# Bias of queries and keys copied into PSUM by ScalarE ahead of the projection, statistics taken for two tiles at once, output projection one round later

## The reference

```python
def attention(x, Wq, bq, Wk, bk, Wv, bv, Wg, bg, Wo, bo):      # x: rmsnorm of the block's input
    q = phi(apply_rope(heads(x @ Wq + bq)))                     # phi(y) = elu(y) + 1
    k = phi(apply_rope(heads(x @ Wk + bk)))
    v = heads(x @ Wv + bv)
    g = heads(sigmoid(x @ Wg + bg))
    # chunks of 64 tokens, in order
    S = S + einsum('bhtd,bhte->bhde', kc, vc)
    Z = Z + kc.sum(axis=2)
    out = gc * (einsum('bhtd,bhde->bhte', qc, S) / (einsum('bhtd,bhd->bht', qc, Z)[..., None] + 1e-06))
    return out @ Wo + bo
```

## Time and profile before

| | |
|---|---|
| median of 3 runs | 2349.87 us (2348.94 to 2350.94) |
| the profiled execution | 2348.44 us, its span 2346.6 us |
| granted TensorE clock, mean over the span | 0.965 of full speed |
| busy over the span | PE 94%, PEld 82%, DVE 71%, ACT 38%, POOL 38% |
| first product of the attention (L1665, tile 0) | 794.00 us from the span's start |
| product L1665 of tile 5 (round 8) | 824.32 us |
| product L1665 of tile 9 (round 12, the first with every step) | 849.95 us |
| product L1665 of tile 31 (round 34) | 997.77 us |
| last score of the router kept | 1035.6 us |

### The profile page before, as it was taken

The page is one execution under the profiler, slowest core; times in us unless marked ns, Lnnn a source line. Parts: engine busy times, 40 slices in busy tenths (PEclk is TensorE's granted clock), DMA queues, the critical chain, the costliest instruction groups (busy, mean ns, idle before and its releaser), DMA issues. The chain is left out here.

```text
span 2346.6 us, 38035 instructions
## 1 busy us (share of the span) xinstructions
PE 2201.3 (94%) x13660; PEld 1929.2 (82%) x13660; DVE 1677.0 (71%) x3543; ACT 901.1 (38%) x1673; POOL 893.6 (38%) x925
## 2 busy tenths in 40 slices
PE   7998999999999599957999999969998999999998
PEld 5887888888889477746899999957887888888887
DVE  6775777777777588855766666646766777777776
ACT  5222333333333477732333333335222333333333
POOL 4211233333332599923444444443202332332332
PEclk9997999999999799968999999989998999999999
DMA  5003354354443411122334444352013444444442
GB/s 183 28 28 123 111 133 131 112 141 129 112 143 78 127 55 42 42 56 83 72 81 84 84 84 85 62 125 90 28 55 120 124 114 140 127 125 123 129 134 46
DMA packets 154108, 228.06 MB, mean 97 GB/s; under 512 B 33344, under 2 KB 104512, under 8 KB 153920
## 3 DMA queue, kind: packets, MB, share of 16 engines
q1 hardware_dynamic: 103664, 158.42, 21.5%
q0 software_dynamic: 39936, 55.93, 13.8%
q10 hardware_dynamic: 10320, 11.27, 1.4%
HBM read 171.16 MB, written 54.39 MB: 96 GB/s over the span
## 5 line engine op out<-in xcount | busy, mean ns | idle before, releaser
L1223 ACT ACTIVATE me_act_f<-me_in,me_bias 128x512 f32<-128x512 f32 (+1 forms) x192 | 119.0, 620 | 291.7 <-PE me_in L148 290.0
L1223 ACT ACTIVATE f2e_silu<-f2e_in,f2e_bias 128x512 f32<-128x512 f32 (+1 forms) x136 | 90.1, 663 | 341.5 <-PE f2e_in L148 293.6
L1223 ACT ACTIVATE f1e_silu<-f1e_in,f1e_bias 128x512 f32<-128x512 f32 (+1 forms) x136 | 90.2, 663 | 341.1 <-PE f1e_in L148 293.3
L146 PE MATMUL f1e_in<-f1e_xt_hi,f1e_w_hi 128*128 128x512 f32 (+1 forms) x544 | 208.9, 384 | 3.6 <-DVE f1e_xt_lo L1283 2.0
L146 PE MATMUL f2e_in<-f2e_xt_hi,f2e_w_hi 128*128 128x512 f32 (+1 forms) x544 | 208.8, 384 | 3.6 <-DVE f2e_xt_lo L1283 2.0
L148 PE MATMUL f2e_in<-f2e_xt_hi,f2e_w_lo 128*128 128x512 f32 (+1 forms) x544 | 208.1, 383 | 0.0
L148 PE MATMUL f1e_in<-f1e_xt_hi,f1e_w_lo 128*128 128x512 f32 (+1 forms) x544 | 207.9, 382 | 0.0
L147 PE MATMUL f2e_in<-f2e_xt_lo,f2e_w_hi 128*128 128x512 f32 (+1 forms) x544 | 207.7, 382 | 0.0
L147 PE MATMUL f1e_in<-f1e_xt_lo,f1e_w_hi 128*128 128x512 f32 (+1 forms) x544 | 207.5, 381 | 0.0
L146 PE MATMUL me_down<-me_w_hi,me_act_hi 128*128 128x256 f32 x640 | 183.4, 287 | 0.0
L147 PE MATMUL me_down<-me_w_lo,me_act_hi 128*128 128x256 f32 x640 | 179.7, 281 | 0.0
(11 more groups left out here) (460 smaller groups left out, 6996.2 us busy)
## 6 DMA issues: line engine op xcount, KB each, us to landing
f_raw<-in_ffn_w SPq DMA_DIRECT2D x256, 384.0 KB, 3.2
m_raw<-in_moe_w SPq DMA_DIRECT2D x64, 256.0 KB, 2.8
f1s_x_all<-in_x SPq DMA_DIRECT2D x8, 512.0 KB, 7.0
after_ffn<-f1s_out SPq DMA_DIRECT2D x8, 512.0 KB, 2.9
after_moe<-ma_x_all SPq DMA_DIRECT2D x32, 128.0 KB, 1.7
m_h<-ma_h SPq DMA_DIRECT2D x32, 128.0 KB, 1.7
f2s_x_all<-after_moe SPq DMA_DIRECT2D x8, 512.0 KB, 9.7
out<-f2s_out SPq DMA_DIRECT2D x8, 512.0 KB, 2.9
```

The source lines that it names most:

```text
L146: pe.matmul(out, lh, rh, start=first, stop=False, skip_group_check=True)
L1223: act.activation(dst[:, st % 2, 0:n], ps_in[st % 2][0][:, 0:n], func, bias=bias[:, b, f:f + 1]).then_inc(silu_done, 1)
```

## The change

The bias of queries and keys no longer comes from a product. ACT copies the bias row (held on all partitions) into `ps_qk` by the new step `set_bias`, and the six matmuls add to it. `set_bias` of tile r stands in the round before its projection, right behind `copy_qk` of tile r - 1, and takes over the wait for DVE's `rotate` of tile r - 1. One matmul of zeros over the bank at the start replaces the setting up of `pick` and `bias_rows`. Mean and variance are taken for two tiles in every second round, and POOL makes scale and shift for both in four operations (before: three for each tile), one round earlier. On PE `project_o` goes from lag 7 at the end of a round to lag 8 behind `turn_q`. On DVE the statistics go to the front, and `feature` goes behind `state1` and `state0`.

```diff
-            def root(r):
...
-                pool.tensor_scalar(mv[:, u, 2:3], mv[:, u, 1:2], EPS, None, ALU.add).then_inc(own_var, 1)
-                pool.wait_ge(own_var, r + 1)
-                pool.tensor_tensor(rs[:, u], mv[:, u, 1:3], neg_half[:], ALU.pow).then_inc(own_pow, 1)
-                pool.wait_ge(own_pow, r + 2)
-                pool.tensor_scalar(shift[:, u], rs[:, u], mv[:, u, 0:1], -1.0, ALU.mult, ALU.mult).then_inc(rs_done, 1)
+            def roots(r):
+                if r % 2 == 0:
+                    pair = slice(r % 4, r % 4 + 2)
+                    pool.wait_ge(stat_done, r + 2)
...
+                    pool.tensor_scalar(neg_mean[:, pair], mv[:, pair, 0], -1.0, None, ALU.mult)
+                    pool.tensor_scalar(mv[:, pair, 2], mv[:, pair, 1], EPS, None, ALU.add).then_inc(own_var, 1)
+                    pool.wait_ge(own_var, r // 2 + 1)
+                    pool.tensor_tensor(rs[:, pair], mv[:, pair, 1:3], neg_half[:], ALU.pow).then_inc(own_pow, 1)
+                    pool.wait_ge(own_pow, r // 2 + 2)
+                    pool.tensor_tensor(shift[:, pair], rs[:, pair], neg_mean[:, pair].unsqueeze(2).to_broadcast([P, 2, 2]),
+                                       ALU.mult).then_inc(rs_done, 1)
...
-            rounds([(10, row_roots), (1, root), (8, residual), (2, add_bo), (3, rotate)])
+            rounds([(10, row_roots), (0, roots), (8, residual), (2, add_bo), (3, rotate)])
...
+            pe.matmul(ps_qk[:], zeros[:, 0:P], zeros[:], start=True, stop=True).then_inc(qk_cleared, 1)
...
                 pe.wait_ge(at_done, r + 1)
-                if r >= 1:
-                    pe.wait_ge(rot_a_done, r)
-                pe.matmul(ps_qk[:], pick[:], bias_rows[:], start=True, stop=False, skip_group_check=True)
+                pe.wait_ge(bias_set, r + 1)
                 project(r, ps_qk, QK, qk_done)
...
-            rounds([(12, score), (6, turn_q), (7, numerators), (5, chunks), (6, last_chunk), (3, project_qk), (7, turn_o),
-                    (11, turn_h), (2, turn_a), (3, project_vg), (7, project_o)])
+            rounds([(12, score), (6, turn_q), (8, project_o), (7, numerators), (5, chunks), (6, last_chunk), (3, project_qk),
+                    (7, turn_o), (11, turn_h), (2, turn_a), (3, project_vg)])
...
+            def set_bias(r):
...
+                if r >= 1:
+                    act.wait_ge(rot_a_done, r)
+                act.copy(ps_qk[:], bias[:, QK]).then_inc(bias_set, 1)
...
-            rounds([(12, keep_score), (6, copy_qt), (4, exp_rot), (3, copy_qk), (7, copy_ot), (11, copy_ht),
-                    (2, split_at), (1, norm), (8, sum_squares), (10, normalise_h), (3, values)], after=(2, round_bias))
+            rounds([(12, keep_score), (6, copy_qt), (4, exp_rot), (3, copy_qk), (2, set_bias), (7, copy_ot), (11, copy_ht),
+                    (2, split_at), (1, norm), (8, sum_squares), (10, normalise_h), (3, values)])
...
-            rounds([(8, add_out), (0, stat), (7, divide), (4, feature), (6, state1), (5, state0), (3, rotate), (7, split_o),
-                    (2, split_low), (3, add_vg_bias)], after=(1, weights_low))
+            rounds([(0, stats_of_pair), (8, add_out), (7, divide), (6, state1), (5, state0), (4, feature), (3, rotate),
+                    (7, split_o), (2, split_low), (3, add_vg_bias)], after=(1, weights_low))
```

More of the change, by code:

```diff
@@ L1455, in attention @@
         wo_hi, wo_lo = s.sb("wo_hi", [P, K, D], F32R), s.sb("wo_lo", [P, K, D], F32R)
-        bias, bias_rows = s.sb("bias", [P, 4 * D]), s.sb("bias_rows", [P, 2 * D], F32R)
-        pick_f, pick = s.sb("pick_f", [P, P]), s.sb("pick", [P, P], F32R)
+        bias = s.sb("bias", [P, 4 * D])
         bo, rope = s.sb("bo", [P, D]), s.sb("rope", [P, Q, 4, DK // 2])
-        zeros, square = s.sb("zeros", [P, K * HW]), s.sb("square", [P, D])
+        zeros, square = s.sb("zeros", [P, 2 * D]), s.sb("square", [P, D])
         x_all, x2_all = s.sb("x_all", [P, T, D]), s.sb("x2_all", [P, T, D])
@@ L1498, in attention @@
                 "o_turned", "ot_done", "wo_done", "x2_done", "sum_done", "total_done"))
-        own_den, own_div, own_var, own_pow, own_ones, own_mean = (
-            s.sem(n) for n in ("own_den", "own_div", "own_var", "own_pow", "own_ones", "own_mean"))
+        own_den, own_div, own_var, own_pow, own_mean = (
+            s.sem(n) for n in ("own_den", "own_div", "own_var", "own_pow", "own_mean"))
         root2_done, h_done, h_turned, ht_done, score_done, score_kept, router_done, spare_out = (
@@ L1619, in _ @@
             for u in range(2):
-                pe.matmul(ps_state[u][:].rearrange("p k c -> p (k c)"), zeros[:, 0:P], zeros[:], start=True, stop=False,
+                pe.matmul(ps_state[u][:].rearrange("p k c -> p (k c)"), zeros[:, 0:P], zeros[:, 0:K * HW], start=True, stop=False,
                           skip_group_check=True)
+            pe.matmul(ps_qk[:], zeros[:, 0:P], zeros[:], start=True, stop=True).then_inc(qk_cleared, 1)
             pe.wait_ge(const_in, 16 * N_CONST)
@@ L1753, in _ @@
                 act.activation(w_hi[:, k], w_raw[:, k], ACT.Copy, scale=scale[:, k:k + 1]).then_inc(w_hi_done, 1)
-            def round_bias():
-                act.wait_ge(bias_in, 16)
-                act.copy(bias_rows[:], bias[:, QK]).then_inc(rows_rounded, 1)
+            def set_bias(r):
+                if r == 0:
+                    act.wait_ge(bias_in, 16)
+                    act.wait_ge(qk_cleared, 1)
+                if r >= 1:
+                    act.wait_ge(rot_a_done, r)
+                act.copy(ps_qk[:], bias[:, QK]).then_inc(bias_set, 1)
             def norm(r):
-                u = r % 2
-                act.wait_ge(rs_done, r + 1)
+                u, q = r % 2, r % 4
+                act.wait_ge(rs_done, r // 2 + 1)
                 if r >= 2:
                     act.wait_ge(a_turned, r - 1)
-                act.activation(x2_all[:, tile(r)], x_all[:, tile(r)], ACT.Identity, bias=shift[:, u, 1:2], scale=rs[:, u, 1:2])
-                act.activation(a[:, u], x_all[:, tile(r)], ACT.Identity, bias=shift[:, u, 0:1], scale=rs[:, u, 0:1]
+                act.activation(x2_all[:, tile(r)], x_all[:, tile(r)], ACT.Identity, bias=shift[:, q, 1:2], scale=rs[:, q, 1:2])
+                act.activation(a[:, u], x_all[:, tile(r)], ACT.Identity, bias=shift[:, q, 0:1], scale=rs[:, q, 0:1]
                                ).then_inc(a_done, 1)
@@ L1848, in _, with stats_of_pair @@
             dve.memset(v1[:], 1.0).then_inc(set_up, 1)
[L1849 to L1865, removed]
+            def stats_of_pair(r):
+                if r % 2 == 0:
+                    if r >= 4:
+                        dve.wait_ge(stat_done, r - 2)
+                    for i in (r, r + 1):
+                        dve.wait_ge(loaded(i), 16)
+                        dve.bn_stats(stats[:, i % 4], x_all[:, tile(i)]).then_inc(stats_done, 1)
+                    wait_apart(dve, stats_done, r + 2)
+                    if r >= 4:
+                        wait_apart(dve, a_done, r - 2)
+                    for i in (r, r + 1):
+                        dve.bn_aggr(mv[:, i % 4, 0:2], stats[:, i % 4]).then_inc(stat_done, 1)
             def split_low(r):
@@ L1957, in scale_router @@
                                       ).then_inc(router_done, 1)
[L1959 to L1962, removed]
             def weights_low():
```

20 lines of the change are left out of this document (7 added, 13 removed).

## The result

The changed kernel takes **2362.6 us** (median of 5 runs, 2359.1 to 2365.1) against 2349.0 us for the kernel before (median of 5, 2345.9 to 2350.9): ratio 1.0058, 95% interval 1.0044 to 1.0073, slower by 13.7 us. The forecast was 2356.3 us, range 2343 to 2363, slower with a chance of 0.56. The direction and the mechanism of the steady rounds were right; the loss was twice the forecast, and the median lies 0.4 us inside the upper end of the range.

What follows compares the result with a forecast made beforehand. POOL's list was taken as the bound, 13.45 us a pair of rounds, PE close behind at 13.02. Terms 7.5 + 1.0 + 1.2 - 0.7 - 2.5 = +6.5 us on the profiled 2348.44 gave a forecast median of 2356.3, range 2343 to 2363.

Steps and rivals of the forecast that it cites:

- steady rounds: Rounds 12 to 34 of the attention: 14.1 us a pair against 13.45, +7.5 us in all, between +5 and +10.
- What bounds the kernel now: In the attention, POOL's own list sets 13.45 us a pair of rounds; PE is close behind at 13.02.
- VectorE's loop: From rotate to rotate through set_bias, ACT's copies, split_at and DVE's list: 7.21 us in the round with statistics.
- TensorE's loop: From rotate to rotate through set_bias, copy_ot, copy_ht and PE's list with the moved project_o: 6.89 us.
- The price of the bias copy: set_bias on ACT, writing 128x512 into PSUM: 0.48 us until the next copy, bounds 0.38 and 0.60.
- Round 7: copy_ot of tile 0 comes behind rotate and set_bias, ahead of all of project_o's start: +1.2 us, bounds 0 and 2.
- The clock: Rival: PE waits some 0.6 us a round and its clock falls, +3 us a round, +70 in all; chance 0.02.
- Rounds 8 to 11: Attention rounds without score and copy_ht: 13.3 us a pair against 12.8, +1.0 us.
- The start: PE's bias_rows wait and slow product go, but the first norm awaits a second tile's statistics: -0.7 us, bounds -1.3 and +0.6.
- The tail: Behind the last projection, score and turn_q stand in PE's wait for split_o; four rounds, -2.5 us.
- the rival of a slowed VectorE: A DVE pass beside a long POOL operation slows the statistics round, +5 us on top: +11 to +16; chance 0.10.
- The faster rival: PE becomes the bound at 12.54 us a pair in the steady rounds: about -13 us, 2337; chance 0.20.

Runs made afterwards that it cites:

- E7: Kernel before with only the statistics and roots of two tiles at once, at the old place in VectorE's order; 2351.5 us, ratio 1.0004.
- E4: Kernel before with only project_o moved one round later, behind turn_q; 2343.7 us, ratio 0.9979.
- R1: Changed kernel run once more, unchanged, for its trace; 2362.9 us.
- R2: Changed kernel run another time, unchanged, for its trace; 2363.4 us.
- E1: Changed kernel with only set_bias moved on ScalarE, from ahead of copy_ot to behind split_at; 2338.0 us, ratio 0.9952.
- E8: Changed kernel with set_bias behind split_at and project_o back at its old place, the round's end; 2341.7 us, ratio 0.9961.
- E3: Kernel before with set_bias alone, ahead of copy_ot, in place of the bias product; 2370.3 us, ratio 1.0095.
- E2: Changed kernel with the bias product back on TensorE and no set_bias, the rest of the change kept; 2343.2 us, ratio 0.9968.
- E5: Changed kernel with set_bias between copy_ht and split_at on ScalarE; 2342.4 us, ratio 0.9968.
- E6: Changed kernel with set_bias between copy_ot and copy_ht on ScalarE; 2353.6 us, ratio 1.0012.

## Why the prediction was right or wrong

- *What bounds the kernel now.* Right: with GpSimd relieved alone (E7) the rounds went from 6.72 to 6.50 us, TensorE's 6.51 of the earlier trace rows. GpSimd's list was taken as fixed at 13.45 us a pair, and in E4 a pair takes 13.13 (910.53 to 923.66, from one L1571 to the second next).
- *The loops.* Right in kind and in place: ACT waits for `ma_rot_a`, DVE for `ma_ot_hi`, PE for `ma_ht`, the rounds alternate. VectorE's loop was 7.21 forecast, 7.16 measured. TensorE's loop was **6.89 forecast, 7.06 measured**, and that is the mis-sized term of the steady rounds: `project_o` at its new place takes 915.88 - 914.99 = 0.89 us until the next matmul against 0.71 taken from the round's end before, the bias copy 0.53 until the next copy against 0.48, `score` and `turn_q` 0.64 against 0.71. (The 0.27 of `copy_ot` is the row of `copy_ht` in the earlier trace rows, 920.06 - 919.79; its own row has 0.51 there. It measured 0.26.) A pair takes 14.25 us on average against 14.1 forecast and 13.45 before, and the 11 pairs between tile 9 and 31 cost 8.9 us, where 11 times the forecast 0.65 is 7.2 (the prediction counted 11.5 pairs).
- *The price of the bias copy.* 0.59 us, by its row L1761; 0.52 to 0.53 until the next copy, inside the bounds of 0.38 and 0.60. The Trainium skill, "ScalarE: Activation LUTs", section "ACT is a hardware spline evaluator", says that ScalarE reaches PSUM with less delay than SBUF. For this shape no run shows it: 0.59 into PSUM, 0.60 into SBUF.
- *Rounds 4 to 7* had no term and cost about 2 us. The loop over `split_at` was priced from round 8 on only; nothing in its sum needed the later steps.
- *Round 7*, forecast +1.2: 1.0 us where the clock stays (R1), 3.5 and 3.9 where it falls. The clock was a rival with 0.02 and was looked for in the steady rounds, where it stayed at 1.00; it fell outside them, from 800 to 815 us, in this round and in the tail. The Trainium skill, "TensorE: Matmul & The Clock Gate", Part 1, says that idle time lowers the clock, and that the number of slow products at a kernel's start differs between runs. Two of the three traces agree with the first, behind a wait of 3.42 us that left the clock at 1.00 in the third; and they show a difference between runs in the middle of a kernel too.
- *Rounds 8 to 11*: tile 5 to 9 cost 1.8 to 2.4 us, forecast +1.0.
- *The start*: -0.1 to -0.5 us, forecast -0.7.
- *The tail*, forecast -2.5: -2.9 in the first trace, +0.6 and +0.2 in R1 and R2. The granted clock of the first 20 us behind `copy_qk` of tile 31 goes with it: 0.91 in the first trace, 0.69 and 0.75 in R1 and R2, 0.81 and 0.82 in the traces of before. E4's gain of 2.6 came at 0.88, so that it isn't the order's alone. At like clocks the tail takes 37.9 us with `project_o` at its old place (E7, 0.68) and 36.5 with it moved (R1, 0.69): some 1.4 us for the order, about half of the forecast; the rest goes with the clock. That the first trace comes close to the forecast is in part luck.
- *The sum.* In the first trace: start -0.14, rounds 4 to 7 2.13, tile 5's round 3.46, to tile 9 1.78, steady 8.87, tail -2.90, together 13.2 us, against +6.5. The misses: steady rounds +1.4, rounds 4 to 7 +2.1, tile 5's round +2.3, rounds 8 to 11 +0.8, the start +0.6, the tail -0.4. In R1 and R2 the steady rounds again cost 8.9 us, and the pieces add to 15.2 and 16.0.
- *The range.* Its upper end came from the rival of a slowed VectorE, which the steady rounds don't show (the division's pass L1932 took 0.42 us, VectorE's loop 7.16). What filled it were the steady rounds' +1.4, rounds 4 to 7 and the clock, of which the last two had no term in the sum. Two of the five runs lie above 2363, so that the median is inside is in part luck.
- *The faster rival* (TensorE becomes the bound, 2337 us, 6.27 us a round) was the right account of what the rest of the change can give: E1 has 6.25 us and 2338 us. The prediction named its condition, that ACT's wait ends before ACT would have come to `copy_ot`; as the change was written, it doesn't.
- *What the profile would show.* As forecast, except that GpSimd's idle time comes in one round of each pair (1.4 and 0.8 us in it), not in every round.

## What to carry to other kernels

An instruction that is put into an in-order list brings its wait along, and the wait is paid by whatever is queued behind it: before adding one, list the readers of the next three or four instructions, and place it behind those that another engine needs this round. The same change was 0.6% slower with the bias copy in one place and 0.5% faster three places on, which needed no other edit. A loop priced from the first round in which all of its steps run misses the rounds before: ask from which round on its two ends exist. And a wait can cost some microseconds more than its length where the clock falls behind it; that differed between executions of one program, so a single trace doesn't price it.

## What the runs showed of the hardware

- The wait ahead of the first `project_o` begins at a granted clock of 1.00 in all thirteen traces. During it or just behind it the clock fell to 0.50, its lower level, in eight traces and stayed at 1.00 in five. The length of this wait doesn't decide it alone: the clock fell with waits of 3.42 (the changed kernel's first trace and R2), 3.36 (E8), 3.08 (E3), 2.88 (E1), 2.46 (E2), 2.10 (E7) and 1.86 us (E5), and stayed with 3.42 (R1), 2.12 and 2.13 (the kernel before), 1.92 (E4) and 1.86 us (E6). In the changed kernel the fall cost 2.5 to 2.9 us in that round. In the steady rounds, with waits of about 0.6 us (1.1 in E3), the clock stayed at 1.00.
- The same small GpSimd instruction takes 0.23 us in E4 and 0.72 in the kernel before. POOL's timeline in E4, then in the kernel before:

```profile
917.75 0.23 POOL L1571 TENSOR_SCALAR ma_mv<-ma_mv 128x1 f32<-128x1 f32 x1
918.06 1.02 POOL L1573 TENSOR_TENSOR ma_rs<-ma_mv,ma_neg_half 128x2 f32<-128x2 f32 x1
```

```profile
917.89 0.72 POOL L1571 TENSOR_SCALAR ma_mv<-ma_mv 128x1 f32<-128x1 f32 x1
```

  In E4 it starts 0.07 us ahead of VectorE's phi (917.82), and the next instruction is the long one (1.02 us). In the kernel before it starts 0.14 us later, when phi has begun at 917.84, and ends 0.08 us behind it. That phi stretches it is only argued. It is why a list of GpSimd's durations from one round is no fixed bound.
